# Shared expert with its weights in the array and the tokens streaming

## The reference, cut to what matters

```python
x = x + xattn(layernorm(x), ctx)                      # B=8, S=128, D=256
h = layernorm(x)
scores = softmax(h @ gate_w.T)                        # 64 experts, top 6 of them, weights rescaled
routed = sum over the 6 experts e of w[t, e] * (silu(g_e) * u_e) @ w_down[e].T    # 176 features each
sgu = h @ ws_gate_up.T                                # the shared expert: 2 x 352 features
shared = (silu(sgu[:, :352]) * sgu[:, 352:]) @ ws_down.T
out = x + routed + shared                             # everything float32
```

## Time and profile before

| | us |
|---|---|
| median of three runs | 316.78 |
| the profiled execution, whole | 316.09 |
| its span, first to last instruction | 314.1 |
| TensorE busy in the span | 264.7 |
| GpSimd busy | 183.7 |
| VectorE busy | 144.1 |
| ScalarE busy | 127.6 |
| mean granted clock of TensorE | 0.937 |

### The profile page before, as it was taken

How to read it: one execution, slowest core, us unless ns; L and a number is a source line. 1 busy time by engine, 2 the same in 40 slices (tenths; PEclk the granted TensorE clock), 3 DMA queues, 4 the chain that set the end, 5 groups by cost and what they waited for, 6 DMA issues and landing times.

```text
span 314.1 us, 6847 instructions
## 1 busy us (share of the span) xinstructions
PE 264.7 (84%) x1698; PEld 230.7 (73%) x1698; DVE 144.1 (46%) x642; ACT 127.6 (41%) x376; POOL 183.7 (58%) x161
## 2 busy tenths in 40 slices
PE   7898766796949989999999999999999999996000
PEld 4485544575727768999999999999999999995000
DVE  3835886564846634443433333333334343343036
ACT  2515352123212254555555555555555455543000
POOL 8202188684774542766665667566657887888000
PEclk9999998977996999999999999999999999999555
DMA  6999999999432365999999999999999999656953
GB/s 177 377 420 428 414 362 389 392 386 333 149 122 105 107 139 140 301 331 322 326 332 334 335 330 334 331 339 330 332 337 337 338 336 310 114 82 118 312 207 134
DMA packets 47196, 89.08 MB, mean 284 GB/s; under 512 B 6508, under 2 KB 32189, under 8 KB 45877
## 3 DMA queue, kind: packets, MB, share of 16 engines
q1 hardware_dynamic: 25413, 61.48, 54.2%
q0 software_dynamic: 12816, 17.12, 26.3%
q10 hardware_dynamic: 8928, 10.04, 9.4%
HBM read 58.08 MB, written 30.54 MB: 282 GB/s over the span
## 4 chain that ended last, share of the span: by engine, by line
PE 57%; issue 14%; POOL 11%; DMA 11%; SPq 2%; DVE 2%; DVEq 1%; ACT 0%; POOLq 0%
PE PS L1118 28%; DMA x_slots<-WA 10%; POOL x_slots L407 9%; PE PS L1130 9%; PE PS L1131 9%; PE PS L986 5%; PE PS L1093 3%; PE PS L1107 2%; DVE X L910 1%; POOL RS L401 1%; DMA acc<-PT,IDR 1%; PE PS L1061 1%; DVE XN L910 1%; POOL HX L429 0%; SPq L248 0%
## 5 line engine op out<-in xcount | busy, mean ns | idle before, releaser
L1118 PEld LDWEIGHTS PS<-XT,WA 128*128 128x128 f32 (+1 forms) x852 | 105.5, 187 | 4.4 <-issue 0.8
L1118 PE MATMUL PS<-XT,WA 128*128 128x128 f32 (+1 forms) x852 | 105.9, 274 | 0.5 <-ACT XT L507 0.5
L444 POOL DMA_INDIRECT acc<-PT,IDR x52 | 81.5, 1567 | 32.8 <-ACT PT L610 14.5
L855 DVE TENSOR_TENSOR AC<-SG,PS 128x128 f32<-128x128 f32 x71 | 20.4, 288 | 97.7 <-ACT SG L583 75.7
L610 ACT ACTIVATE PT<-PS,WT 128x256 f32<-128x256 f32 x70 | 33.2, 474 | 34.0 <-issue 15.2
L407 POOL DMA_INDIRECT x_slots<-HX,SLOT x36 | 35.6, 988 | 16.8 <-issue 9.7
L1130 PE MATMUL PS<-WA,AC 128*128 128x256 f32 x140 | 41.8, 380 | 0.0
L1131 PE MATMUL PS<-WB,AC 128*128 128x256 f32 x140 | 41.6, 379 | 0.0
L444 POOL DMA_INDIRECT out_rows<-PT,IDR x18 | 28.2, 1568 | 21.5 <-DVE IDR L844 9.4
L507 ACT COPY XT<-PS 128x256 f32<-128x256 f32 x73 | 27.1, 372 | 18.6 <-PE PS L986 9.5
L582 ACT ACTIVATE SG<-PS 128x128 f32<-128x128 f32 x71 | 19.7, 277 | 29.4 <-PE PS L1118 25.6
(11 more groups left out here) (144 smaller groups left out, 314.5 us busy)
## 6 DMA issues: line engine op xcount, KB each, us to landing
WA<-in_wa SPq DMA_DIRECT2D x71, 496.0 KB
x_slots<-WA SPq DMA_DIRECT2D x1, 8704.0 KB, 30.2
VXG<-x_slots ACTq DMA_DIRECT2D x57, 136.0 KB
WB<-in_wb SPq DMA_DIRECT2D x71, 48.0 KB
acc<-ZERO SPq DMA_DIRECT2D x2, 1152.0 KB
CT<-in_ctxT SPq DMA_DIRECT2D x2, 512.0 KB, 6.1
X<-in_x SPq DMA_DIRECT2D x2, 512.0 KB, 6.3
out_rows<-X SPq DMA_DIRECT2D x8, 128.0 KB
```

The costliest lines, as they stand in the source:

```text
L444: pool.indirect_dma_start(acc[u % NACC], bass.IndirectOffsetOnAxis(ap=IDR[:, u:u + 1], axis=0), YS[:, u % YR, :], None, compute_op=ALU.add ...
L855: v.tensor_tensor(AC[:, w % 2, 0, :], SG[:, w % 2, 0, :], PS[:, 4 + w % 2, 0:128], ALU.mult)
L1118: last = mm(PS[0:n, (4 if c == 2 else 2) + w % 2, c % 2 * 128:(c % 2 + 1) * 128], WA[:, base:base + n], XT[:, w % 2, k, :], start=(k == 0) ...
```

## The change

The weights go into the array and the tokens stream. Gate and up then come out with features on the partitions and tokens along the free axis, which is how the second product wants them, so the turn and its copy are left out. The 352 features are cut into chunks of 128, 128 and 96. `SAC` gets two buffers, and VectorE's write of it waits for an earlier second product (`s_sd`) rather than for the turn. tanh, `SSG` and `SAC` work on 3 x 128 = 384 elements per partition rather than 352. `WSD` is loaded as 128 partitions x 3 x 256, the last 32 feature rows filled with zeros.

```diff
-FC = 88
+SC = (128, 128, SF - 256)
+SW = 128 * len(SC)
...
-        WSD = sb("WSD", [FC, SF // FC, D])
+        WSD = sb("WSD", [128, len(SC), D])
...
 ScalarE
-                if 0 <= i - 4 < B:
-                    s = i - 4
-                    act.wait_ge(s_st, s + 1)
-                    ge(act, s_sd, s)
-                    nc.scalar.copy(SACT[:], PS[0:FC, STB, :].rearrange(...)).then_inc(s_stc, 1)
-                    nc.scalar.activation(SEX[:], PS[:, GATE, 0:SF], ACT.Tanh, scale=0.5).then_inc(s_sex, 1)
+                    nc.scalar.activation(SEX[:], PS[:, GATE, 0:SW], ACT.Tanh, scale=0.5).then_inc(s_sex, 1)
 VectorE
-                    ge(dve, s_st, s)
-                    v.scalar_tensor_tensor(SAC[:], SSG[:], 0.5, PS[:, UP, 0:SF], ALU.mult, ALU.mult)...
+                    ge(dve, s_sd, s - 1)
+                    v.scalar_tensor_tensor(SAC[:, s % 2, :], SSG[:], 0.5, PS[:, UP, 0:SW], ALU.mult, ALU.mult)...
 TensorE
-                if 0 <= i - 4 < B:
-                    s = i - 4
-                    pe.wait_ge(s_sact, s + 1)
-                    ge(pe, s_stc, s)
-                    for c in range(SF // FC):
-                        last = tr(PS[0:FC, STB, c * 128:(c + 1) * 128], SAC[:, c * FC:(c + 1) * FC], IDN)
-                    last.then_inc(s_st, 1)
...
-                        for k in range(KD):
-                            last = mm(PS[:, GATE + g, 0:SF], HT[:, k, s * S:(s + 1) * S], WSG[:, k, g * SF:(g + 1) * SF], ...)
+                        for c, n in enumerate(SC):
+                            for k in range(KD):
+                                last = mm(PS[0:n, GATE + g, c * 128:(c + 1) * 128], WSG[:, k, g * SF + c * 128:g * SF + c * 128 + n],
+                                          HT[:, k, s * S:(s + 1) * S], start=(k == 0), stop=(k == KD - 1))
...
-                    pe.wait_ge(s_stc, s + 1)
+                    pe.wait_ge(s_sact, s + 1)
                     ge(pe, s_shc, s)
-                    for c in range(SF // FC):
-                        last = mm(PS[:, SDB, 0:D], SACT[:, c, :], WSD[:, c, :], ...)
+                    for c, n in enumerate(SC):
+                        last = mm(PS[:, SDB, 0:D], SAC[0:n, s % 2, c * 128:(c + 1) * 128], WSD[0:n, c, :], ...)
```

More of the change, by code:

```diff
@@ L146, in program @@
         WARM = sb("WARM", [128, 1])
[L147 to L150, removed]
+        SEX = sb("SEX", [128, SW])
+        SSG = sb("SSG", [128, SW])
+        SAC = sb("SAC", [128, 2, SW])
         OVF = sb("OVF", [128, COLS])
@@ L168, in program @@
         ZROW = WA[:, (R - 3) * WROW:(R - 3) * WROW + ZROWS * ROW]
-        RANK, ZB, WO, STB, LOGIT, GATE, UP, SDB = range(8)
+        RANK, ZB, WO, _, LOGIT, GATE, UP, SDB = range(8)
         PS = ctx.enter_context(nc.psum_tensor("PS", [128, 8, 512], f32))
@@ L181, in program @@
         s_lg, s_nm, s_ex, s_m, s_rk, s_slot = (sem(n) for n in ("s_lg", "s_nm", "s_ex", "s_m", "s_rk", "s_slot"))
-        s_sgu, s_sex, s_sact, s_st, s_stc, s_sd, s_shc = (
-            sem(n) for n in ("s_sgu", "s_sex", "s_sact", "s_st", "s_stc", "s_sd", "s_shc"))
+        s_sgu, s_sex, s_sact, s_sd, s_shc = (sem(n) for n in ("s_sgu", "s_sex", "s_sact", "s_sd", "s_shc"))
         s_v1, s_r1, s_vg, s_rg, s_nb, s_yn, s_v2, s_r2 = (
@@ L537, in _ @@
                                    PS[:, LOGIT, 256:512].rearrange("p (k n) -> p k n", k=KD)).then_inc(s_htc, 1)
-                if 0 <= i - 4 < B:
-                    s = i - 4
-                    act.wait_ge(s_st, s + 1)
-                    ge(act, s_sd, s)
-                    nc.scalar.copy(SACT[:], PS[0:FC, STB, :].rearrange("p (c n) -> p c n", c=SF // FC)).then_inc(s_stc, 1)
                 if 0 <= i - 5 < B:
@@ L831, in _ @@
                     dve.wait_ge(s_sex, s + 1)
-                    ssg = tick(v.scalar_tensor_tensor(SSG[:], SEX[:], 1.0, PS[:, GATE, 0:SF], ALU.add, ALU.mult))
+                    ssg = tick(v.scalar_tensor_tensor(SSG[:], SEX[:], 1.0, PS[:, GATE, 0:SW], ALU.add, ALU.mult))
                     if b is not None:
@@ L835, in _ @@
                     need(ssg)
-                    ge(dve, s_st, s)
-                    v.scalar_tensor_tensor(SAC[:], SSG[:], 0.5, PS[:, UP, 0:SF], ALU.mult, ALU.mult).then_inc(s_sact, 1)
+                    ge(dve, s_sd, s - 1)
+                    v.scalar_tensor_tensor(SAC[:, s % 2, :], SSG[:], 0.5, PS[:, UP, 0:SW], ALU.mult, ALU.mult).then_inc(s_sact, 1)
                 if k == B - 1:
@@ L1053, in _ @@
                     last.then_inc(s_ht, 1)
-                if 0 <= i - 4 < B:
-                    s = i - 4
-                    pe.wait_ge(s_sact, s + 1)
-                    ge(pe, s_stc, s)
-                    if s == 0:
-                        pe.wait_ge(s_wrc, 4)
-                    for c in range(SF // FC):
-                        last = tr(PS[0:FC, STB, c * 128:(c + 1) * 128], SAC[:, c * FC:(c + 1) * FC], IDN)
-                    last.then_inc(s_st, 1)
                 if i < B:
@@ L1091, in _ @@
                     for g in range(2):
-                        for k in range(KD):
-                            last = mm(PS[:, GATE + g, 0:SF], HT[:, k, s * S:(s + 1) * S], WSG[:, k, g * SF:(g + 1) * SF],
-                                      start=(k == 0), stop=(k == KD - 1))
+                        for c, n in enumerate(SC):
+                            for k in range(KD):
+                                last = mm(PS[0:n, GATE + g, c * 128:(c + 1) * 128], WSG[:, k, g * SF + c * 128:g * SF + c * 128 + n],
+                                          HT[:, k, s * S:(s + 1) * S], start=(k == 0), stop=(k == KD - 1))
                     last.then_inc(s_sgu, 1)
@@ L1103, in _ @@
                         rows(0, 1)
-                    pe.wait_ge(s_stc, s + 1)
+                    pe.wait_ge(s_sact, s + 1)
                     ge(pe, s_shc, s)
-                    for c in range(SF // FC):
-                        last = mm(PS[:, SDB, 0:D], SACT[:, c, :], WSD[:, c, :], start=(c == 0), stop=(c == SF // FC - 1))
+                    for c, n in enumerate(SC):
+                        last = mm(PS[:, SDB, 0:D], SAC[0:n, s % 2, c * 128:(c + 1) * 128], WSD[0:n, c, :],
+                                  start=(c == 0), stop=(c == len(SC) - 1))
                     last.then_inc(s_sd, 1)
@@ L1190 @@
         "wsg": chunk(a["L0_ffn_ws_gate_up"].T, 128),
-        "wsd": chunk(a["L0_ffn_ws_down"].T, FC),
+        "wsd": chunk(np.concatenate([a["L0_ffn_ws_down"].T, np.zeros((SW - SF, D), a["L0_ffn_ws_down"].dtype)]), 128),
         "cst": shape_constants(),
```

## The result

| | before | changed | ratio, 95% interval |
|---|---|---|---|
| first comparison, median of 6 each | 316.55 us | 323.15 us | 1.023, 1.018 to 1.028 |
| again on chip 13 | 316.01 | 324.88 | 1.022, 1.012 to 1.032 |
| again on chip 8 | 304.56 | 305.26 | 1.001, 0.998 to 1.004 |

A time is the median of all executions; a ratio leaves out those that lie over 1.5% above the fastest of their kernel. The forecast was 316.2 with 318.9 as its upper end; the change is slower by 2.3%. But the third line is as much the result as the first: chips differ. On some, both kernels run 11 us faster or more, and there the change costs nothing measurable.

The account below looks back on a forecast made before the run. GpSimd's scatters bound 39 to 89 us, then TensorE, then VectorE at the last SAC, then TensorE's tiles. Terms +0.1 - 0.6 + 0 - 0.1 + 0 = -0.6 us gave 316.2 us against a 316.78 median; range 313.4 to 318.9.

Parts of the forecast that it names:

- Costs of the parts: TensorE per block: gate and up +0.29 us, turn -0.44, second product -0.43, together -0.58.
- My fourth rival: Gate and up's 24 instructions take 0.124 us each, not 0.111: +0.3 a block, within the forecast's range; no separate chance.
- Zero fill +0.1: WSD's load grows by 32 KB ahead of the x_slots fill in the same queue, so scatters start 0.1 us later.
- GpSimd's waits -0.6: 39 to 89 us: GpSimd's two waits on TensorE shorten, middle of 0 and -1.2 us.
- 89 to 102 us, 0: TensorE stretch partly at half clock: gate and up +0.44, product behind it -0.5, together taken as 0.
- block 6, -0.1: 102.5 to 107.1 us, one block: turn -0.44, gate and up +0.29, wider passes +0.1; written as -0.1 us.
- The end, 0: After the last SAC: first tile begins 2.2 us earlier, but the third tile's late rows turn that into waiting, gain 0.
- early rows: Second rival: third tile's rows land near 114.4 us, so the 2.2 us count: 314.0 us, chance 0.18.
- the clock: First rival: waiting for rows behind the first tile brings a 3.4 us half-clock stretch, +1.7 us: 317.9 us, chance 0.28.
- What bounds the pipeline: From 39 to 89 us GpSimd's scatters bound; TensorE's or ScalarE's savings count only against its two waits.
- The third rival: TensorE's late signals in the pipeline move: one fewer gives 313.2 us, one added 319.2; chance 0.20.
- one more: One added late signal of TensorE, or one in a worse place, costs 3 us: 319.2 us, chance 0.08.

Follow-up runs that it names:

- run 11: Not a label of a run: the words belong to "both kernels run 11 us faster or more", a time difference on some chips.
- r1: The changed kernel run again on chip 8, beside a kernel before of 304.56 us: 305.26 us, ratio 1.001.
- r5: The kernel before itself, unmodified, run on chip 11 for its trace: 304.04 us.
- r8: The kernel before with 16 more one-column TensorE instructions per block ahead of gate and up, on chip 13: 330.15 us, ratio 1.046.
- e4: The kernel before with 48 increments of an unused semaphore by SyncE in each of eight pipeline steps, on chip 5: 334.26 us, ratio 1.058.
- e5: The kernel before with turn and second product in three chunks (128, 128, 96) instead of four of 88, on chip 6: 306.23 us, ratio 1.006.
- r4: The kernel before without the four turns and their copy, second product reading unturned SAC, on chip 8: 304.60 us, ratio 0.999.

## Why the prediction was wrong

- **Costs of the parts**: right. Gate and up went from 2.53 to 2.82 us, the +0.29 that was said; the product from 1.89 to 1.46, the -0.43. My fourth rival, +0.61, did not come.
- **Zero fill +0.1**: nothing; the first scatter stands at 39.30 before and 39.31 now.
- **GpSimd's waits -0.6**: the failed step. It took the late signals as fixed in number and place, and only asked whether they would end earlier. The change made them longer: four waits of 2.41, 1.03, 5.29 and 1.03 us stand where 1.38 and 3.35 stood, +5.0 instead of -0.6. Eighty more instructions on TensorE were priced by their time alone, and their price on such a chip is what they add to the holds.
- **89 to 102 us, 0**, and **block 6, -0.1**: by the balance the last block's ranks are 4.71 later, so this stretch gives back 0.3 of the 5.0: its hold of 4.34 us stands where one of 3.87 stood. The block behind it is shorter by 0.43.
- **The end, 0**: on the first chip +3.55, the same failed step once more, since the fourth hold stands there. On chips without holds the rest of the term can be seen, in the chip-11 trace of before and the chip-8 trace of the change, one execution each. Before:
```profile
104.55 1.49 PE L1118 MATMUL PS<-XT,WA 128*128 128x128 f32 x12
106.44 0.44 PE L986 MATMUL PS<-CST,VXG 128*128 128x128 f32 x2 [0.39 <-DMA VXG<-x_slots]
107.69 1.56 PE L1118 MATMUL PS<-XT,WA 128*128 128x128 f32 x12 [0.82 <-ACT XT L507]
```
Changed:
```profile
102.73 1.49 PE L1105 MATMUL PS<-XT,WA 128*128 128x128 f32 x12
105.88 0.44 PE L980 MATMUL PS<-CST,VXG 128*128 128x128 f32 x2 [1.66 <-DMA VXG<-x_slots]
106.86 1.57 PE L1105 MATMUL PS<-XT,WA 128*128 128x128 f32 x12 [0.54 <-ACT XT L506]
```
The first tile is 1.82 us earlier (2.2 said), the third tile's rows come late (1.66 us of waiting, about 2 said), and the second tile begins 0.83 earlier. Of that 0.81 is one scatter of 1.77 instead of 0.96 us in the trace of before. So the gain is eaten by the rows, as forecast, and "early rows" did not come. Nor did the clock fall in this execution, as its stretch behind the wait shows; but it is the fastest of ten, and the experiments give reason to think that it fell in six others:
```profile
106.86:109.40 2.54, 2.54 (x19) 2.44 (x20) 0.85 (x5) 0.80 (x3) 0.00 (x0) 1.00 0.38 92
```
- **What bounds the pipeline**: right, and stronger than I wrote. Without holds GpSimd goes from 43 us to the last scatter with some 0.3 us or less between two operations, in r1 as in r5, whose timeline is this:
```profile
59.63 1.17 POOL L407 DMA_INDIRECT x_slots<-HX,SLOT  x1 [0.19 <-issue]
...
67.91 1.16 POOL L407 DMA_INDIRECT x_slots<-HX,SLOT  x1 [0.20 <-issue]
...
76.18 1.16 POOL L407 DMA_INDIRECT x_slots<-HX,SLOT  x1 [0.20 <-issue]
```
8.28 us a block. Nothing that TensorE saves or adds up to 16 narrow instructions a block comes through, which is why the right column of the table stands at 1.00. That the change is near the forecast there is partly luck: the waits of GpSimd from which I took -0.6 do not exist there.
- **The third rival** had the place but not the law. It gave "one more" hold 3 us and 0.08, and held against it that three runs lay within 0.08 us. That was chance, as the later runs show, and it could say nothing on what holds do when the program changes. Its other figure was good: it put all holds with their half clock at up to 11 us, and the kernel before takes 304 to 305 us where it has none. The trace of before already had only 265 of 373 records; I had not counted them.

## What to carry to other kernels

Where a trace has waits marked "remote" behind signals of work long done, count the semaphore records first. If many are missing, as in all eight such traces here, suspect holds, and price a change that splits wide matmuls into narrow ones by its count (here 0.09 to 0.11 us each), not by its columns. Time such a change on a chip whose trace has all records before judging it; and ahead of a change to TensorE's share, see whether another engine, here GpSimd with 0.3 us between scatters, goes without a gap: then what TensorE saves is worth nothing there.

## What the runs showed of the hardware that I had not expected

- The same kernel takes 316 us on chips 5 and 13 and in the first comparison, and 304 to 305 on chips 6, 8 and 11; a change is to be compared with a kernel before that ran beside it on the same chip.
- A matmul instruction of one column with one stationary column takes 0.034 us with its load (16 in 0.54 us, r8).
- Under holds SyncE's increments slow down as well, from 0.06 us each to between 0.21 and 0.23 (e4, 48 in 10.1 to 11.2 us).
- The clock after like waits differs: behind 1.53 + 0.77 us idle e5's granted clock was 0.58, behind 1.42 + 0.68 r4's was 0.66, behind 1.66 + 0.54 r1's was 1.00.
- SyncE's increments take 0.06 us each, 48 in 2.8 to 3.1 us, when not held.
